# A graph attention layer on one core: half of the one-hot rows compared from PSUM on VectorE, half made on ScalarE, and the maximum chain on other tiles

## What is computed

```python
feats = relu(x @ w1 + b1) @ w2 + b2                     # 64 per node
x_cat = concat([feats[row], feats[col], elem[:, None]]) # 129 per edge
hid   = relu(x_cat @ a1 + ab1)
e1    = leaky_relu(hid @ a2 + ab2, 0.2)
w     = exp(e1 - max(e1))
pooled  = segment_sum(w[:, None] * feats[col], row)
row_sum = segment_sum(w, row) + 1e-10
head    = pooled / row_sum[:, None]
# all heads side by side, then layernorm(x + heads)
```

## Time and profile before

| what | us |
|---|---|
| median of 3 runs | 4968.95 |
| the runs | 4963.43 to 4972.03 |
| the profiled execution, its own time | 4966.92 |
| its span in the profile | 4965.1 |

### The profile page before, as it was taken

The page is one execution under the profiler, slowest core; times in us unless marked ns, Lnnn a source line. Parts: engine busy times, 40 slices in busy tenths (PEclk is TensorE's granted clock), DMA queues, the critical chain, the costliest instruction groups (busy, mean ns, idle before and its releaser), DMA issues.

```text
span 4965.1 us, 128744 instructions
## 1 busy us (share of the span) xinstructions
PE 3966.2 (80%) x20790; PEld 2368.7 (48%) x20791; DVE 4349.6 (88%) x25374; ACT 3585.4 (72%) x10903; POOL 3251.4 (65%) x3927
## 2 busy tenths in 40 slices
PE   1588989989986888888888888888888888888870
PEld 1355555555545544555544545555445544455440
DVE  8799999999995888888888888888888888888888
ACT  1587777877865777777777777777777777777774
POOL 5366566666664776666666667666666666676654
PEclk9799999999998999999999999999999999999995
DMA  2133333333336777777777777777777777777757
GB/s 83 42 84 77 73 86 79 75 80 78 78 80 193 218 216 216 216 217 216 216 215 217 214 214 219 214 216 215 216 213 215 216 218 214 216 219 212 212 162 207
DMA packets 266916, 851.80 MB, mean 172 GB/s; under 512 B 107916, under 2 KB 109584, under 8 KB 266861
## 3 DMA queue, kind: packets, MB, share of 16 engines
q0 software_dynamic: 169920, 673.54, 49.0%
q1 hardware_dynamic: 63543, 160.18, 10.8%
q10 hardware_dynamic: 33398, 17.49, 1.4%
HBM read 739.10 MB, written 111.90 MB: 171 GB/s over the span
## 4 chain that ended last, share of the span: by engine, by line
DVE 19%; ACT 19%; PE 16%; issue 14%; DVEq 2%; ACTq 0%; DMA 0%; POOL 0%; POOLq 0%; SPq 0%
DVE z L1568 10%; PE psum L988 9%; ACT psum L1178 8%; ACT z L1187 6%; PE psum L976 3%; DVE acc L1622 3%; ACT onehot L1215 2%; ACT onehot_t L1206 2%; DVE onehot_b L1581 2%; PE psum L1011 1%; DVE head_max L1600 1%; DVEq L462 1%; PE psum L955 1%; DVE z L1695 1%; DVE z L1688 1%
## 5 line engine op out<-in xcount | busy, mean ns | idle before, releaser
L764 POOL DMA_INDIRECT z<-qf_table,rec x1664 | 1605.5, 965 | 1029.0 <-PE psum L976 634.3
L988 PE MATMUL psum<-p_win,onehot_t 128*128 x9984 | 1681.6, 285 | 340.4 <-ACT psum L1178 321.6
L1178 ACT ACTIVATE psum<-z 128x258 f32<-128x258 f32 x3328 | 1259.9, 380 | 767.7 <-DVE z L1568 728.1
L1568 DVE SCALAR_TENSOR_TENSOR z<-psum,a_b 128x129 f32<-128x129 f32 x6656 | 1621.4, 282 | 16.5 <-PE psum L988 10.2
L988 PEld LDWEIGHTS psum<-p_win,onehot_t 128*128 128x128 bf16 x9984 | 974.2, 98 | 1224.1 <-issue 887.0
L976 PE MATMUL psum<-z,onehot 128*128 128x260 f32 x3328 | 1139.6, 425 | 221.5 <-issue 214.9
L1187 ACT ACTIVATE z<-z 128x64 f32<-128x64 f32 x3328 | 912.0, 334 | 0.0
L1622 DVE TENSOR_TENSOR acc<-acc,psum 125x260 f32 x1664 | 694.6, 417 | 65.4 <-PE psum L976 43.7
L693 POOL DMA_INDIRECT sorted_rows<-z x300 | 479.9, 1600 | 403.2 <-DVE z L1460 313.0
L976 PEld LDWEIGHTS psum<-z,onehot 128*128 128x128 f32 x3328 | 510.6, 193 | 336.2 <-issue 281.8
L750 POOL TENSOR_TENSOR z<-z 128x256 f32<-128x256 f32 x832 | 537.6, 647 | 27.2 <-ACT z L1195 14.7
(11 more groups left out here) (216 smaller groups left out, 4622.1 us busy)
## 6 DMA issues: line engine op xcount, KB each, us to landing
p_table<-acc SPq DMA_DIRECT2D x100, 338.6 KB
p_win<-p_table SPq DMA_DIRECT2D x100, 338.6 KB
z<-qf_table,rec POOLq DMA_INDIRECT x1664, 4.3
qf_table<-acc SPq DMA_DIRECT2D x75, 339.5 KB
acc<-in_x_dram SPq DMA_DIRECT2D x25, 448.0 KB
z<-in_x_dram SPq DMA_DIRECT2D x20, 560.0 KB
out_dram<-z ACTq DMA_DIRECT2D x20, 560.0 KB
qf_table<-z SPq DMA_DIRECT2D x25, 339.5 KB
```

Of the source, the lines that this page charges most:

```text
L764: pool.indirect_dma_start(out=z_t[:, o + j, :], out_offset=None, in_=qf_table, in_offset=bass.IndirectOffsetOnAxis(ap=rec[:, o + j, 3:4].b ...
L988: mm = pe.matmul(z_half(slot, u), onehot_t[:, j, :], p_flat[:, bass.ds((turn_at % 2) * (3 * ZW) + (part * ZW + u * HALF), HALF)], start=Fa ...
L1178: act.activation(z_half(slot, u), z_t[:, slot, u * HALF:(u + 1) * HALF], ACT.Copy).then_inc(s_seed[u], 1)
L1568: op = dve.scalar_tensor_tensor(out=z_t[:, slot, h * AT:(h + 1) * AT], in0=z_half(slot, h // 2)[:, h % 2 * AT:(h % 2 + 1) * AT], scalar=0. ...
```

## The change

1. The one-hot rows are made in fp32 at once, in the ring onehot; the bf16 copy onehot_b, the bf16 identity and ScalarE's onehots are gone.
2. Tiles 4 to 7 of the next superblock are compared on VectorE, one between the third and the fourth dot of the tile of the same number. The running numbers are read from PSUM: they are written once ahead of the loop into the unused columns of banks 1 and 3. The compare waits for sum_up of the same tile two steps back, because its slot is used again.
3. Tiles 0 to 3 are made on ScalarE: distance gives |row - number| for one tile, one behind each seed of tiles 4 and 5; rows gives relu(1 - distance) for all four behind the first seed of tile 6.
4. elem_parts writes into onehot, in two halves, behind gathers 3 and 7. turn is an fp32 transpose of onehot; its second half moves from tile 1 to tile 2, and take_turned to ScalarE's tile 3 and to behind the second seed of tile 7.
5. max_t moves from tile 2 to tile 1 on TensorE; max_to_all stays behind tile 3. new_shift and shifted move from tile 2 to tile 3 on VectorE.
6. GpSimd weights five tiles, 0 to 4, ScalarE three. GpSimd does tiles 0 and 1 behind gathers 6 and 7, and 2, 3 and 4 behind gathers 0, 1 and 2 of the next step. ScalarE's weightings are one half behind each seed of tiles 0 to 2.
7. exps moves from tile 4 to tile 6, load_records from tile 6 to tile 7.

The core of the diff:

```diff
-    POOL_W = [0, 1, 2, 3]
-    ACT_W = [4, 5, 6, 7]
+    POOL_W = [0, 1, 2, 3, 4]
+    ACT_W = [5, 6, 7]
...
+        def numbers(slot):
+            return psum[:, slot % 2 * 2 + 1, HALF:HALF + WN]
...
-                    pool.tensor_copy(onehot_b[:, :, WN:P], rec_b[:, o:o + SB, 2:5]).then_inc(s_elem_b, 1)
+                def elem_parts(u):
+                    at = o + u * HALF_SB
+                    pool.tensor_copy(onehot[:, at:at + HALF_SB, WN:P], rec_b[:, at:at + HALF_SB, 2:5]).then_inc(s_elem, 1)
...
-            weighed = {0: [(-2, POOL_W[3])], 5: [(-1, POOL_W[0])], 6: [(-1, POOL_W[1])], 7: [(-1, POOL_W[2])]}
+            weighed = {6: [(-1, 0)], 7: [(-1, 1)], 0: [(-2, 2)], 1: [(-2, 3)], 2: [(-2, 4)]}
...
-                        mm = pe.matmul(psum[:, 6, j * P:(j + 1) * P], onehot_b[:, u * HALF_SB + j, :], ident_h[:, :], start=True, stop=True)
+                        mm = pe.transpose(psum[:, 6, j * P:(j + 1) * P], onehot[:, ((k + off) * SB + u * HALF_SB + j) % RING, :], ident[:, :])
...
-                    if j == 1 and live(i, k, 0):
+                    if j == 2 and live(i, k, 0):
                         turn(0, 1)
-                    if j == SB // 4 and live(i, k, -1):
+                    if j == 1 and live(i, k, -1):
                         max_t()
-                    if j == SB // 4 + 1 and live(i, k, -1):
+                    if j == 3 and live(i, k, -1):
                         max_to_all()
...
+                def distance(off, j):
+
+                    at = (k + off) % SPB * SB + j
+                    if j == 0:
+                        act.wait_ge(s_rec[(k + off) % SPB], i * 16 + ((k + off) // SPB + 1) * 16)
                     if live(i, k, off - 3):
+                        act.wait_ge(s_agg, tile(off - 3, j) + 1)
+                    op = act.activation(onehot[:, at, 0:WN], iota_row[:, :], ACT.Abs, scale=-1.0, bias=rec[:, at, 0:1])
+                    if j == HALF_SB - 1:
+                        op.then_inc(s_row_dist, 1)
+
+                def rows(off):
+
+                    at, n = (k + off) % SPB * SB, i * SPB + (k + off)
+                    act.wait_ge(s_row_dist, n + 1)
+                    act.activation(onehot[:, at:at + HALF_SB, 0:WN], onehot[:, at:at + HALF_SB, 0:WN], ACT.Relu, scale=-1.0,
+                                   bias=ones_f[:, 0:1]).then_inc(s_rows_act, 1)
...
+                behind = {(0, 0): [(weight, -2, 5, 0)], (0, 1): [(weight, -2, 5, 1)], (1, 0): [(weight, -2, 6, 0)], (1, 1): [(weight, -2, 6, 1)],
+                          (2, 0): [(weight, -2, 7, 0)], (2, 1): [(weight, -2, 7, 1)], (3, 0): [(take_turned, 0, 1)],
+                          (4, 0): [(distance, 1, 0)], (4, 1): [(distance, 1, 1)], (5, 0): [(distance, 1, 2)], (5, 1): [(distance, 1, 3)],
+                          (6, 0): [(rows, 1)], (6, 1): [(exps, -1)], (7, 0): [(load_records, 2)], (7, 1): [(take_turned, 1, 0)]}
...
+            for slot in range(2):
+                dve.tensor_copy(numbers(slot), iota_row[:, :]).then_inc(s_acc_zero, 1)
...
                 def compare(j):
 
-                    if j % HALF_SB == 0:
+                    slot = ((k + 1) * SB + j) % RING
+                    if j == HALF_SB:
                         dve.wait_ge(s_rec[(k + 1) % SPB], i * 16 + ((k + 1) // SPB + 1) * 16)
-                        if live(i, k, 0):
-                            dve.wait_ge(s_onehot, sbn(0) * 2 + (j // HALF_SB + 1))
-                            dve.wait_ge(s_oht_mm, sbn(0) * 2 + (j // HALF_SB + 1))
-                    op = dve.tensor_scalar(onehot_b[:, j, 0:WN], iota_row[:, :], rec[:, (k + 1) % SPB * SB + j, 0:1], None, ALU.is_equal)
+                    if live(i, k, -2):
+                        dve.wait_ge(s_agg, tile(-2, j) + 1)
+                    op = dve.tensor_scalar(onehot[:, slot, 0:WN], numbers(j), rec[:, slot, 0:1], None, ALU.is_equal)
...
-                         2: [(-1, new_shift), (-1, shifted)]}
+                         3: [(-1, new_shift), (-1, shifted)]}
...
+                        if n == H - 1 and j >= HALF_SB and live(i, k, 1):
+                            compare(j)
                         if live(i, k, 0):
                             dot(j, n)
```

More of the change, by code:

```diff
@@ L103, in gnn_layer @@
         before = sb("before", [P, P], BF16)
-        iota_row = sb("iota_row", [P, WN], BF16)
-        ident_h = sb("ident_h", [P, P], BF16)
+        iota_row = sb("iota_row", [P, WN])
         iota_win = sb("iota_win", [P, CH, W], BF16)
@@ L318, in gnn_layer @@
         s_rec = [sem(f"s_rec{n}") for n in range(SPB)]
-        s_rows_b = sem("s_rows_b")
-        s_elem_b = sem("s_elem_b")
-        s_onehot = sem("s_onehot")
+        s_row_dist = sem("s_row_dist")
+        s_rows_act = sem("s_rows_act")
+        s_rows_dve = sem("s_rows_dve")
+        s_elem = sem("s_elem")
         s_oht_mm = sem("s_oht_mm")
@@ L405, in gnn_layer @@
         N_PARTS = 5
-        N_TAB_STEPS = 9
+        N_TAB_STEPS = 8
         EMPTY_W = CHUNKS // P * SF
@@ L775, in step @@
                         keep_shift()
-                    if j == 2 and live(i, k, 1):
-                        elem_parts()
+                    if j % HALF_SB == HALF_SB - 1 and live(i, k, 1):
+                        elem_parts(j // HALF_SB)
                     for off, own in weighed.get(j, []):
@@ L802, in _ @@
         def _(pe):
-            pe.wait_ge(s_const, 21)
+            pe.wait_ge(s_const, 20)
             def count_windows(g):
@@ L995, in turn @@
                     n = i * SPB + (k + off)
-                    pe.wait_ge(s_rows_b, n * 2 + (u + 1))
-                    pe.wait_ge(s_elem_b, n + 1)
+                    pe.wait_ge([s_rows_act, s_rows_dve][u], n + 1)
+                    pe.wait_ge(s_elem, n * 2 + (u + 1))
                     since(pe, s_oht, n * 2 + u)
                     for j in range(HALF_SB):
-                        mm = pe.matmul(psum[:, 6, j * P:(j + 1) * P], onehot_b[:, u * HALF_SB + j, :], ident_h[:, :], start=True, stop=True)
+                        mm = pe.transpose(psum[:, 6, j * P:(j + 1) * P], onehot[:, ((k + off) * SB + u * HALF_SB + j) % RING, :], ident[:, :])
                     mm.then_inc(s_oht_mm, 1)
@@ L1058, in _ @@
             act.wait_ge(s_weights, N_W)
-            act.wait_ge(s_const, 20)
+            act.wait_ge(s_const, 19)
             act.wait_ge(s_tables, 1)
@@ L1177, in seed @@
                     since(act, [s_dot_one, s_dot][u], tile(0, j) - 1)
+                    if u and isinstance(i, int) and tile(0, j) < 2:
+                        act.wait_ge(s_rows_dve, 1)
                     act.activation(z_half(slot, u), z_t[:, slot, u * HALF:(u + 1) * HALF], ACT.Copy).then_inc(s_seed[u], 1)
@@ L1220, in load_records @@
                                   rec_d[:, bass.ds((i * SPB + (k + off)) * (SB * 4), SB * 4)]).then_inc(s_rec[kn], 16)
[L1222 to L1226, removed]
-                          (4, 0): [(weight, -2, d, 1)], (4, 1): [(exps, -1)],
-                          (6, 0): [(load_records, 2)], (7, 0): [(take_turned, 1, 0)]}
+                behind = {(0, 0): [(weight, -2, 5, 0)], (0, 1): [(weight, -2, 5, 1)], (1, 0): [(weight, -2, 6, 0)], (1, 1): [(weight, -2, 6, 1)],
+                          (2, 0): [(weight, -2, 7, 0)], (2, 1): [(weight, -2, 7, 1)], (3, 0): [(take_turned, 0, 1)],
+                          (4, 0): [(distance, 1, 0)], (4, 1): [(distance, 1, 1)], (5, 0): [(distance, 1, 2)], (5, 1): [(distance, 1, 3)],
+                          (6, 0): [(rows, 1)], (6, 1): [(exps, -1)], (7, 0): [(load_records, 2)], (7, 1): [(take_turned, 1, 0)]}
                 for j in range(SB):
@@ L1516, in _ @@
                 lambda: dve.tensor_copy(win_tab[WIN_AT[1]:WIN_AT[1] + 1, :].rearrange("p (s j) -> p s j", j=4), halves[WIN_AT[1]:WIN_AT[1] + 1, :, 1, :]),
-                lambda: dve.memset(onehot[:, :, WN:P], 0.0),
                 lambda: dve.memset(end_prev[:, :], 1),
@@ L1544, in _ @@
             dve.wait_ge(s_acc_zero, 1 + BULK)
-            dve.wait_ge(s_start, 1)
+            dve.wait_ge(s_z_mm, 1)
+            for slot in range(2):
+                dve.tensor_copy(numbers(slot), iota_row[:, :]).then_inc(s_acc_zero, 1)
+            dve.wait_ge(s_acc_zero, 3 + BULK)
             def step(i, k):
@@ L1646, in step @@
                         add_sums(j)
-                    if live(i, k, 1):
-                        for own in {3: [0, 1], 4: [2, 3], 5: [4, 5], 6: [6, 7]}.get(j, []):
-                            compare(own)
             pipeline(dve, step)
```

15 lines of the change are left out of this document (2 added, 13 removed).

## The result

The changed kernel takes 4744.13 us (median of four runs, 4731.88 to 4751.4) against 4968.7 us before: a ratio of 0.9546, with a 95% interval from 0.9525 to 0.9568. It is faster by 225 us; 379 had been forecast, and 4744 lies in the range of 4430 to 4760.

What follows compares the result with a forecast made beforehand. VectorE's work plus two maximum-chain waits bound the 15.72 us step. After: GpSimd 13.4 + 0.1 records + 0.4 mutual waits = 13.9 us; over 208 steps 379 us saved, 4967 to 4588, said as 4590, range 4430 to 4760.

Steps and rivals of the forecast that it cites:

- Maximum chain: VectorE's waits for the shift (1.10 us a step) and the heads' maximum (0.21) go; bounds nothing and 1.31.
- Compares: On VectorE, eight bf16 compares (1.9 us a step) become four fp32 ones from PSUM (0.84): 1.1 gained, bounds 0 and 1.6.
- GpSimd: Fullest engine after the change: 12.51 us a step plus 0.65 for tile 4's weighting and 0.23 for copies, 13.4.
- 13.4 + 0.1 + 0.4 = 13.9: Forecast step in us: GpSimd's work and issue idle, waits for records, and waits of near-equal engines on each other.
- rows 8: Profile rows cited for GpSimd: a gather starts 0.16 us behind another instruction and 0.30 behind a gather.
- Records: Load issued in ScalarE's tile 7, about 2 us later, delays gather 0: 0.1 us a step, bounds 0 and 2.
- ScalarE and the DMA engines: Neither bounds the loop: ScalarE falls from 11.73 to 11.2 us a step; DMA share rises from 0.74 to 0.84.
- TensorE: Fp32 transposes replace eight bf16 turns: +0.4 us, 13.5 us a step as the profile counts.
- the dear compares: Rival on VectorE: PSUM compares keep the eight's price, 1.9 us; step 14.5 us, 4713 us in all; chance 0.06.
- the compare's wait in place of the old ones: Rival on VectorE: each compare stands 0.4 us for sum_up, 1.6 us a step; 4776 us in all; chance 0.16.
- The rival in which GpSimd's waits are a loop: Gathers wait for sums, sums for weightings: GpSimd's 3.1 us waits stay, step 16.5 us, 5129 us in all; chance 0.05.

Runs made afterwards that it cites:

- opening the loop at three places: Changed kernel with load_records behind tile 6's first seed, sum_up of tile 7 in its own step, weights of tile 1 ahead of gather 7: 4648.47 us.
- both details mended and two orders changed: Changed kernel with records at tile 6, four tiles weighted on GpSimd one tile sooner, and tile 7's sum in its own step: 4541.62 us, 0.9129.

## Why the forecast was right in its way and too high in its size

*Maximum chain*: right. The waits at L1610 and L1600 went as said, and alone they give 215 us of the 272 reckoned. TensorE's new wait at max_t, which was priced at nothing, is 0.36 us a step.

*Compares*: both prices were too low, and the difference came out by luck. A new compare was priced at a dot's 0.21 us; it lasts 347 ns and its busy share is 236.2/680 = 0.35, so four are 1.4 us a step and not 0.84. The eight old ones were put at 1.9 us from two pairs (the 0.47 us called the mean of the old ones is that of a pair), but the groups of the kernel before in 2000 to 4500 us have them at 400.2/159 = 2.5:

```profile
L1581 DVE TENSOR_SCALAR onehot_b<-iota_row,rec 128x125 bf16<-128x125 bf16 x1272 | 400.2, 367 | 0.0
...
L1592 DVE SCALAR_TENSOR_TENSOR e_val<-e_val 128x32 f32<-128x32 f32 x159 | 76.9, 483 | 0.0
...
L1614 DVE TENSOR_TENSOR e_sh<-e_val,shift 128x32 f32<-128x32 f32 x159 | 29.8, 187 | 0.0
```

So the compares did become 1.1 us cheaper, as forecast. VectorE's work as a whole fell by less, 0.5 us a step against the kernel before (13.53 to 13.06) and 0.87 against the chain alone, and none of it reached the time. Part of the difference is that other instructions became longer: e_sh went from 187 to 453 ns, and leaky, which was stretched before, from 483 to 552. The page GPSIMD Engine Reference of the Trainium skill, section Specifications, says that GpSimd's SBUF interfaces are shared with VectorE, with contention for VectorE instructions in a two-port performance mode or with two SBUF inputs. For the compares the traces agree: the one from SBUF is stretched beside a weighting (568 ns after 284), the one from PSUM is not. That e_sh and leaky, which have two SBUF inputs, are stretched by the same is not shown: in the changed kernel a gather (for leaky a gather and a short copy), and not a weighting, runs beside most of them.

*GpSimd*: the step that failed is the sum "13.4 + 0.1 + 0.4 = 13.9", which came out at 14.7. The engine was named rightly and its work sized rightly (11.6 us). The rest of the sum was not. Its first term, work and "issue" idle, is 11.6 + 2.1 = 13.7 instead of 13.4; the records are 32.5/170 = 0.19 instead of 0.1; and the 0.4 for engines losing on each other is 0.75 us of waits for sums. That makes 14.6 of the 14.7. I took the 0.16 and 0.30 us that rows 8 show as what a gather's start costs; a gather that waits for its sum starts 0.8 us behind it, and idle under "issue" grew from 1.62 to 2.1 us. No run changes that 0.8 us itself. What the runs show is that work put ahead of the gathers that wait gains time (35 us for one weighting ahead of gather 7, 60 for all five one tile sooner), and that less work on GpSimd gains more: four weightings instead of five give 83 us (4692.75 to 4610.02), and a better place for them a further 35 (to 4575.02).

*Records*: priced at 0.1 us a step within bounds of 0 and 2; it cost 51 us, 0.25 a step. The bound was right, and the value was taken from waits of a load that still had a tile to spare. It was also a mean: the eight waits of the kernel before all lie between 3143 and 3521 us, and 17 of the 22 of the changed kernel between 3400 and 4200.

*ScalarE and the DMA engines* were no bound, as said. ScalarE works 11.63 us where 11.2 was forecast (a distance takes 385 ns, where 0.29 us was taken), and took a fourth weighting back without harm. TensorE counts 12.5 us where 13.5 was forecast.

*The rivals*: two gave times nearer to 4744 than the forecast's 4590, the dear compares (4713) and the compare's wait in place of the old ones (4776), and neither by its mechanism. That wait is 0.34 us a step and not 1.6. The new compares cost 1.4 us, half-way between the 0.84 taken and the rival's 1.9, but the old ones cost more too, and taking 0.87 us of VectorE's work away did not shorten the step. The rival in which GpSimd's waits are a loop names a path that is there, sums that wait for weightings (0.67 us a step), but its condition is not: it decides from 2.3 us of GpSimd's waits left, and 0.75 are left.

*Luck*: the total lies in the range, but the chain alone gives the same time within the error. The part forecast for the rest of the change, some 107 of the 379 us, did not come.

Left open: what sets the 14 us of the changed kernel in full. Moving tile 7's sum changed nothing alone, opening the loop at three places left 14.1 us, and taking work off GpSimd or moving it to a better place went further; several chains of nearly one length would fit this, but no run here names them.

## What to carry to other kernels

Time the parts of a change apart: here a two-line edit of an order made the whole gain, while the rework around it took 0.87 us a step of work off VectorE, the busiest engine, and gave it back through two details, a load issued one tile later and one more task on an in-order queue. With both details mended and two orders changed, the kernel takes 4.6% less than with the chain alone (4762 to 4542 us). Before an engine's waits are counted as room, look at how long it needs to start again behind what it waits for; a gap of 0.16 us seen where nothing was awaited says nothing of that. And when a step is moved later, ask for its first reader's slack in the stretch where it already waits, not on the mean.

## What had not been expected of the hardware

Some gathers start late for no cause that the trace shows, in both kernels, and their numbers are a multiple of 90 apart. Two of them in the changed kernel, the 384th and the 474th gather of the loop, 163 us apart:

```profile
2238.02 0.97 POOL L763 DMA_INDIRECT z<-qf_table,rec  x1 [2.57 <-issue]
...
2398.87 0.61 POOL L749 TENSOR_TENSOR z<-z 128x256 f32<-128x256 f32 x1
2401.28 0.97 POOL L763 DMA_INDIRECT z<-qf_table,rec  x1 [1.80 <-issue]
```

The first is a gather 7, the second a gather 1. In the kernel before, the 384th and the 474th are late as well, at 2298.25 and 2474.03 us, so it goes by the number of gathers and not by time. Through the loop the late ones that can be seen are 90 or 180 gathers apart in the changed kernel. It was not tried what makes it.

Of the 170 e_sh of the changed kernel in 2000 to 4500 us, 119 take over 0.3 us, and 112 of these end within 0.03 us of the end of the gather beside them, though GpSimd's spans are rough. Why is not shown.

The late start of a gather behind the sum it waits for (0.82 us at the median, in both kernels) was the other surprise, and the one that the forecast's sum missed.
